# A recurrent attention block on one Trainium2 core: the order of gates and activations in its two halves

## The chip, the core and the metric

The kernel is one program on one core of a Trainium2 chip (trn2). The metric is the device time of one execution in microseconds (us), lower is better; the median of three executions before the change is 1480.96 us.

## The reference, cut to what matters

The whole program is a four-layer network on an input of 4 sequences of 256 tokens with 256 features. Each layer is a conditioning step, an attention block, another conditioning step and a feed-forward block. The change touches only the attention block of the second layer, which is a gated linear recurrence (RG-LRU) behind a causal convolution:

```python
def _rg_lru(x, wa, ba, wx, bx, lam):
    r = sigmoid(einsum('bld,ed->ble', x, wa) + ba)      # recurrence gate
    i = sigmoid(einsum('bld,ed->ble', x, wx) + bx)      # input gate
    log_a = -8.0 * r * softplus(lam)
    a = exp(log_a)
    mult = sqrt(maximum(1.0 - exp(2.0 * log_a), 0.0))
    b = mult * (i * x)
    # h[t] = a[t] * h[t-1] + b[t], along the sequence
# block: h = silu(x @ w1.T + b1); c = causal convolution of h with 4 taps, 320 -> 320 channels;
#        y = _rg_lru(c, ...) @ w2.T + b2;  x = x + y
```

The inner width is 320 channels. They are held as three channel groups of 128, 128 and 64 partitions.

## The kernel before, in words

The program is a chain of stages, one function per block of the network. Between two stages all engines meet. The stage of this case is `stage_l1_attn(l)` with l = 2; `stage_l1_ffn(3)` follows it. Each engine has its own instruction stream inside a stage, written out by hand; the streams meet only at semaphores, and every engine works strictly in the order written.

The 1024 tokens are two **halves** h = 0, 1 of 512 tokens (two sequences each), which fill one PSUM bank of 512 float32 columns. The unit of TensorE work is a `product`: one accumulation group into one bank, with one count of the semaphore `done` at its end. There are 28 of them, numbered by `group[0]`; product g uses bank g mod 8, so from g = 8 on it waits until ScalarE has evacuated product g - 8 (`evac` at least g - 7). In order:

- g 0 to 5: first projection w1, both halves, three channel groups each, 2 matmuls per product;
- g 6 to 11 (`G_CONV` = 6): the convolution, first half, then second half, 10 matmuls per product;
- g 12 to 23 (`G_GATE` = 12): the gates, per half and per channel group first the recurrence gate (`rec`), then the input gate (`inp`), 3 matmuls per product;
- g 24 to 27 (`G_OUT` = 24): the output w2, per half two blocks of 128 output features, 3 matmuls per product, behind `scan_ready`, which counts halves.

A float32 matmul of 512 columns stands in the trace as two instructions, so a convolution product is 20 of them, a gate or output product 6.

**ScalarE (ACT)** evacuates: Silu for w1 (L1122 to L1126), Identity into `conv` (L1135), Sigmoid into `rec` and `inp` (L1142). After all gates of both halves it computes, per half, three Exp into `mul` (L1149) and three Exp in place in `rec` (L1153), then for both halves three Sqrt each in `mul` (L1159). A change of function that needs another table puts an ACT_TABLE_LOAD in front.

**VectorE (DVE)** takes 1 minus (L1177) after the exponentials, then per half, behind `root_ready` and `ix_ready`, three products `mul` times `inp` (L1184) and six scans (L1189, the recurrence of 256 steps, one per channel group and sequence), and at the end four additions of output and bias to the residual `xT` (L1195).

**GpSimd (POOL)** multiplies gate and input, `inp` times `conv` (L1102), per half once all six gates of that half are evacuated.

Beside this the stage carries the work of the **next conditioning step**, 8 pieces of (128 features x 256 tokens). For each piece DVE computes `uk` and four scans (L151 to L158) and later a maximum, a reciprocal and a product (L192 to L198); ACT one Exp (`piece_act`, L169) behind DVE's `uk`; POOL two sums and a product (L175 to L180). DVE does them all (`block_dve`) before anything of the recurrence; ACT spreads its eight Exp over the six convolution evacuations. DVE's `uk` of piece i stands behind its `piece_finish` of piece i - 2, and two buffers take turns.

Of the kernel before, what the change touches and what calls it, by code (L numbers as in the profile page):

```python
# [14 lines left out]
P = 128  # L15
# [5 lines left out]
NP = CH * NB  # L21
# [18 lines left out]
ALU = mybir.AluOpType  # L40
ACT = mybir.ActivationFunctionType
# [49 lines left out]
def build_program(nc, io):  # L91
# [38 lines left out]
    dstep, astep, pstep = steps["dve"], steps["act"], steps["pool"]  # L130
# [6 lines left out]
    def vec(name, i=0):  # L137
        return vecs[:, ds(VEC[name][0] + i, 1)]
# [916 lines left out]
    def stage_l1_attn(l):  # L1055
        TP = T + 6
        RC = 3
        rows = (P, P, R1 - 2 * P)
        with ExitStack() as st:
            def sb(n, shape, dt=F32):  # L1060
# [13 lines left out]
            lam = sb("lam", [P, 6, RC])  # L1074
            ps = st.enter_context(nc.psum_tensor("R_ps", [P, 8, HALF], F32))
            names = ("ld_w1 ld_conv ld_gate ld_w2 zeroed done evac lam_ln "
                     "lam_ready a2_ready one_minus root_ready ix_ready scan_ready out_read").split()
            s = {n: sem("R_" + n) for n in names}
            block = st.enter_context(nc.Block())
            G_CONV, G_GATE, G_OUT = 6, 12, 24  # L1080
            h512 = lambda h: slice(h * HALF, (h + 1) * HALF)

            @block.sync
# [7 lines left out]
            @block.gpsimd  # L1091
            def _(pool):
                pool.memset(hid[:, :, :, :], 0.0)
                pstep.link(pool.memset(hid2[:, :, :], 0.0))
                pstep.link(pool.memset(conv[64:P, 2, :], 0.0))
                pool.memset(inp[64:P, 2, :], 0.0).then_inc(s["zeroed"], 1)
                block_pool(pool, l + 1)
                for h in range(2):
                    pool.wait_ge(s["evac"], G_GATE + 6 * (h + 1))
                    for f in range(RC):  # L1100
                        n = rows[f]
                        ins = pool.tensor_tensor(inp[0:n, f, h512(h)], inp[0:n, f, h512(h)], conv[0:n, f, h512(h)], ALU.mult)  # L1102
                        if f == RC - 2:
                            pstep.link(ins)
                    ins.then_inc(s["ix_ready"], 1)
                    pool.wait_ge(s["ix_ready"], h + 1)

            @block.scalar
            def _(act):
                condition_act(act, sig)  # L1110

                astep.link(act.activation(lam[:, 0, :], vecs[:, VEC["lam"][0]:VEC["lam"][0] + RC], ACT.Abs))
                astep.link(act.activation(lam[:, 1, :], lam[:, 0, :], ACT.Exp, scale=-1.0))
                act.activation(lam[:, 2, :], lam[:, 1, :], ACT.Ln, bias=1.0).then_inc(s["lam_ln"], 1)
                act.wait_ge(s["zeroed"], 1)
                pair = lambda x: x.rearrange("p (b t) -> p b t", b=2)
                for h in range(2):
# [11 lines left out]
                for h in range(2):  # L1129
                    for f in range(RC):  # L1130
                        g, n = G_CONV + 3 * h + f, rows[f]
                        for i in range(NP * (g - G_CONV) // 6, NP * (g - G_CONV + 1) // 6):
                            piece_act(act, l + 1, i, i % 2)
                        act.wait_ge(s["done"], g + 1)
                        act.activation(conv[0:n, f, h512(h)], ps[0:n, g % 8, :], ACT.Identity,  # L1135
                                       bias=vec("convb", f)[0:n, :]).then_inc(s["evac"], 1)
                for h in range(2):
                    for f in range(RC):
                        for j, (dst, b) in enumerate(((rec, "ba"), (inp, "bx"))):
                            g, n = G_GATE + 6 * h + 2 * f + j, rows[f]  # L1140
                            act.wait_ge(s["done"], g + 1)
                            act.activation(dst[0:n, f, h512(h)], ps[0:n, g % 8, :], ACT.Sigmoid,  # L1142
                                           bias=vec(b, f)[0:n, :]).then_inc(s["evac"], 1)
                act.wait_ge(s["lam_ready"], 1)
                act.wait_ge(s["evac"], G_OUT)
                for h in range(2):
                    for f in range(RC):
                        n = rows[f]
                        astep.mark(act.activation(mul[0:n, f, h512(h)], rec[0:n, f, h512(h)], ACT.Exp, scale=lam[0:n, 5, f:f + 1]))  # L1149
                    astep.wait()  # L1150
# [3 lines left out]
                    ins.then_inc(s["a2_ready"], 1)  # L1154
                for h in range(2):
                    act.wait_ge(s["one_minus"], h + 1)
                    for f in range(RC):
                        n = rows[f]
                        ins = act.activation(mul[0:n, f, h512(h)], mul[0:n, f, h512(h)], ACT.Sqrt, bias=1.0)  # L1159
                    ins.then_inc(s["root_ready"], 1)  # L1160
                next_sigmoid(act, l + 1)

            @block.vector
            def _(dve):
# [8 lines left out]
                for h in range(2):  # L1173
# [5 lines left out]
                for h in range(2):  # L1179
                    dve.wait_ge(s["root_ready"], h + 1)  # L1180
                    dve.wait_ge(s["ix_ready"], h + 1)
                    for f in range(RC):
                        n = rows[f]
                        dstep.link(dve.tensor_tensor(mul[0:n, f, h512(h)], mul[0:n, f, h512(h)], inp[0:n, f, h512(h)], ALU.mult))  # L1184
                    for f in range(RC):
                        n = rows[f]
                        for b in (2 * h, 2 * h + 1):
                            c = slice(b * T, (b + 1) * T)
                            ins = dve.tensor_tensor_scan(inp[0:n, f, c], rec[0:n, f, c], mul[0:n, f, c], 0.0, ALU.mult, ALU.add)  # L1189
                    ins.then_inc(s["scan_ready"], 1)  # L1190
# [8 lines left out]
            def _(pe):  # L1199
                group = [0]  # L1200

                def product(pairs, n):

                    g = group[0]
                    group[0] += 1
                    if g >= 8:
                        pe.wait_ge(s["evac"], g - 7)
                    for i, (w, x) in enumerate(pairs):
                        ins = pe.matmul(ps[0:n, g % 8, :], w, x, start=(i == 0), stop=(i == len(pairs) - 1))
                    ins.then_inc(s["done"], 1)  # L1210
# [14 lines left out]
                pe.wait_ge(s["ld_gate"], 16)  # L1225
                for h in range(2):
                    pe.wait_ge(s["evac"], G_CONV + 3 * (h + 1))
                    for f in range(RC):
                        c = slice(f * P, f * P + rows[f])
                        for j in range(2):  # L1230
                            product([(wgate[:, j, k, c], conv[:, k, h512(h)]) for k in range(RC)], rows[f])
                pe.wait_ge(s["ld_w2"], 16)
                for h in range(2):
                    pe.wait_ge(s["scan_ready"], h + 1)
                    for m in range(CH):
                        product([(w2[:, k, m * P:(m + 1) * P], inp[:, k, h512(h)]) for k in range(RC)], P)

    def stage_l1_ffn(l):  # L1240
# [879 lines left out]
```

## Time and profile before

| | |
|---|---|
| executions before | 1476.59, 1480.96, 1480.99 us; median 1480.96 |
| profiled execution, its own time | 1482.23 us |
| its span, first to last instruction | 1480.4 us |
| mean granted TensorE clock | 0.911 of 2.4 GHz |
| busy: PE, DVE, ACT, POOL | 79%, 66%, 40%, 39% of the span |
| the stage of this case | from 582.4 to 716.1 us of the span |

All times in views are microseconds from the start of the span. A view of windows gives busy time and instruction count of each engine in each stretch, and PEclk, the granted TensorE clock as a share of 2.4 GHz, where 0.50 is the lower of its two levels, 1.2 GHz. A timeline lists instructions in order of time with like neighbours merged: start, length, engine, line, operation, count, and in brackets how long the engine had been idle and who released it. A busy share over the whole span is a mean over stages with different limits.

### The profile page before, as it was taken

The page shows a single profiled execution, that of the slowest core. Times are in us where ns is not written, and L with a number is a line of the kernel's source. Part 1 is how long each engine was busy: PE and PEld are TensorE (multiplying, and loading weights), DVE is VectorE, ACT ScalarE, POOL GpSimd, SP SyncE. Part 2 cuts the span into 40 slices and gives each one's busy share as a digit, 9 for nine tenths or more (in the row PEclk, how much of TensorE's full clock was granted, in tenths as well). Part 3 has the DMA queues.
Part 4 walks back from the last instruction along what each step waited for, and adds up shares of the span by engine and source line. Part 5 has one row for each costly group of instructions (what it writes and reads, how often), then busy time and mean ns, then how long its engine had stood idle before and what let it go on. Part 6 is the DMA issues. An engine that isn't in the chain of part 4 may idle for free. (4 is left out here: it accounts for less than half of the span.)

```text
span 1480.4 us, 16753 instructions
## 1 busy us (share of the span) xinstructions
PE 1166.2 (79%) x5816; PEld 847.8 (57%) x5816; DVE 980.0 (66%) x1934; ACT 593.0 (40%) x1405; POOL 583.7 (39%) x462
## 2 busy tenths in 40 slices
PE   0177898989788887994779963999999966069997
PEld 0044555555557665431568853888888832047876
DVE  7757777877738987662513444888888858964345
ACT  2145556555635545225124522333333335123333
POOL 4346656565605651432051233444444411504520
PEclk9978999999979999997669995999999987569999
DMA  1121121021111102000423522110000000011101
GB/s 65 46 57 46 34 65 43 20 75 29 30 30 43 36 22 89 25 1 0 183 85 131 189 70 77 36 37 30 29 29 29 4 12 24 0 30 50 51 22 61
DMA packets 28979, 71.65 MB, mean 48 GB/s; under 512 B 4960, under 2 KB 14688, under 8 KB 26080
## 3 DMA queue, kind: packets, MB, share of 16 engines
q1 hardware_dynamic: 26320, 65.34, 14.4%
q0 software_dynamic: 1536, 4.20, 1.0%
q8 instruction: 47, 0.77, 0.2%
q10 hardware_dynamic: 1040, 1.05, 0.2%
q14 instruction: 36, 0.29, 0.1%
HBM read 55.89 MB, written 4.19 MB: 41 GB/s over the span
## 5 line engine op out<-in xcount | busy, mean ns | idle before, releaser
L175 POOL TENSOR_TENSOR sums<-scans 128x512 f32<-128x512 f32 x64 | 86.1, 1345 | 327.9 <-DVE scans L158 189.8
L504 ACT ACTIVATE probs<-ps_s,stats 128x256 f32<-128x256 f32 (+1 forms) x256 | 104.3, 419 | 102.2 <-DVE stats L571 102.1
L665 PE MATMUL ps_p<-xin,wkvq 128*128 128x512 f32 x148 | 75.9, 638 | 69.4 <-DMA wkvq<-w_l0a_dram 69.4
L450 POOL TENSOR_TENSOR probs<-probs,stats 128x512 f32<-128x512 f32 x64 | 67.5, 1055 | 127.8 <-DVE stats L577 127.8
L195 DVE RECIPROCAL sums<-sums 128x256 f32<-128x256 f32 x64 | 112.1, 1751 | 1.8
L571 DVE CUSTOM_DVE_ANT_0 ps_s<-ps_s,mask 128x256 f32<-128x256 f32 (+1 forms) x256 | 83.5, 387 | 23.9 <-PE ps_s L691 23.8
L180 POOL TENSOR_TENSOR sums<-sums,terms 128x512 f32<-128x512 f32 x64 | 86.7, 1355 | 4.4
L839 POOL TENSOR_TENSOR L3hid<-L3hid,L3sig 128x1024 f32<-128x1024 f32 x17 | 46.1, 2718 | 87.6 <-ACT L3sig L892 49.8
L665 PEld LDWEIGHTS ps_p<-xin,wkvq 128*128 128x128 f32 x148 | 26.9, 202 | 89.5 <-DMA wkvq<-w_l0a_dram 67.0
L1723 PE MATMUL K_ps_kvp<-K_wqkv_hi,K_xin_hi 128*128 128x256 f32 x256 | 75.1, 293 | 0.0
L1723 PE MATMUL K_ps_kvp<-K_wqkv_lo,K_xin_hi 128*128 128x256 f32 x256 | 72.5, 283 | 0.0
L1723 PE MATMUL K_ps_kvp<-K_wqkv_hi,K_xin_lo 128*128 128x256 f32 x256 | 72.4, 283 | 0.0
L1628 ACT ACTIVATE K_ks<-K_ps_kvp 128x256 f32<-128x256 f32 x64 | 24.7, 385 | 110.1 <-PE K_ps_kvp L1723 110.1
L701 PE MATMUL ps_t<-ident,probs 128*128 128x128 f32 x128 | 38.7, 302 | 37.0 <-ACT probT L511 23.0
L169 ACT ACTIVATE terms<-uk 128x256 f32<-128x256 f32 x64 | 26.5, 417 | 97.6 <-DVE uk L151 97.5
L691 PE MATMUL ps_s<-kr,qr 64*128 64x256 f32 (+1 forms) x512 | 61.5, 361 | 4.0 <-DVE qr L565 2.1
L717 PEld LDWEIGHTS ps_o<-probT,vtok 128*64 128x64 f32 x512 | 32.0, 140 | 49.5 <-issue 31.0
L1489 PE MATMUL E_ps<-E_dT,E_fc 128*128 128x256 f32 x256 | 59.1, 392 | 0.8 <-ACT E_dT L1344 0.8
L958 DVE TENSOR_TENSOR L3hid<-L3actg,L3ps_u 128x512 f32<-128x512 f32 x34 | 23.3, 687 | 54.4 <-ACT L3actg L886 54.4
L451 POOL TENSOR_TENSOR probs<-probs,stats 128x256 f32<-128x256 f32 x64 | 59.0, 923 | 0.0
L717 PE MATMUL ps_o<-probT,vtok 128*64 128x256 f32 (+1 forms) x512 | 57.6, 347 | 0.7 <-ACT oT L519 0.7
L691 PEld LDWEIGHTS ps_s<-kr,qr 64*128 64x128 f32 x512 | 45.9, 194 | 20.4 <-issue 10.9
(377 smaller groups left out, 3563.0 us busy)
## 6 DMA issues: line engine op xcount, KB each, us to landing
E_fc<-l_fc_dram SPq DMA_DIRECT2D x16, 1024.0 KB, 6.6
qswap<-qraw SPq DMA_DIRECT2D x64, 128.0 KB, 2.3
K_wqkv<-l_wqkv_dram SPq DMA_DIRECT2D x16, 384.0 KB, 3.3
L3wgu<-L_w_dram SPq DMA_DIRECT2D x17, 256.0 KB, 2.6
L0wgu<-L_w_dram SPq DMA_DIRECT2D x14, 256.0 KB, 2.6
wkvq<-w_l0a_dram SPq DMA_DIRECT2D x4, 768.0 KB, 4.5
L3wdn<-L_w_dram SPq DMA_DIRECT2D x17, 128.0 KB, 2.0
wo<-w_l0a_dram SPq DMA_DIRECT2D x4, 512.0 KB, 3.8
```

Source lines behind the costliest of these rows:

```text
L175: pstep.mark(pool.tensor_tensor(sums[:, k, :, :], scans[:, k, :, 0, :], scans[:, k, :, 1, :], ALU.add))
L180: pool.tensor_tensor(sums[:, k, :, :], sums[:, k, :, :], terms[:, k, :, :], ALU.add).then_inc(sums_ready, 1)
L195: dstep.mark(dve.reciprocal(den, den))
L450: pool.tensor_tensor(p1, p1, rs[:, 0:2].unsqueeze(2).to_broadcast([P, 2, T]), ALU.mult)
L451: pool.tensor_tensor(p0, p0, rs[:, 2:4].unsqueeze(2).to_broadcast([P, 2, P]), ALU.mult).then_inc(s["norm_done"], 1)
L504: ins = act.activation(dst[:, i % 2, :], src[:, i % 2, :], ACT.Exp, bias=stats[:, g % 4, 4 + i:5 + i], scale=-1.0, accum_out=stats[:, g % ...
L571: ins = dve.tensor_tensor_reduce(out=view, in0=view, in1=m, scale=-1.0, scalar=-NEG, op0=ALU.add, op1=ALU.min, accum_out=stats[:, g % 4, 4 ...
L665: ins = pe.matmul(ps[:, :], w[:, k, :], xin[:, k, h * HALF:(h + 1) * HALF], start=(k == 0), stop=(k == CH - 1))
L691: ins = pe.matmul(view[:, r, :], qr[h, (4 * c + m) % 2, b * T + tile * P:b * T + tile * P + P], kr[h, c % 2, b, 0:n], start=True, stop=True)
L717: ins = pe.matmul(o, vtok[:, c % 2, 2 * b + key, 64 * r:64 * r + 64], probT[:, g % 2, r, 0:256] if key == 0 else probT[:, g % 2, r, 256:38 ...
L1489: ins = pe.matmul(ps[:, h, i * CAP:(i + 1) * CAP], fc1[:, k, c, f:f + P], dT[:, c, ds(e * CAP, CAP)], start=(c == 0), stop=(c == CH - 1))
L1723: ins = pe.matmul(ps_kvp[:, h, a, :], x[:, k, t:t + P], w[:, j // 2, k, P:3 * P], start=(k + m == 0), stop=(k == CH - 1 and m == 2))
```

## The change

All of it lies in `stage_l1_attn`.

- TensorE: after the convolution of half 0 come the six gate products of half 0, then the convolution of half 1 and its gates. Within a half the three recurrence gates lead and the three input gates follow. `G_CONV` becomes (6, 15), `G_GATE` (9, 18). The first output product of each half waits for the scans channel group by channel group.
- ScalarE: the same order, with the exponentials of half 0 (`powers`) and its square roots (`roots`) placed among the evacuations of half 1's convolution. In half 1 the exponentials come after the recurrence gates and ahead of the input gates. The eight Exp of the conditioning pieces are spread from the start of the stage to the end of half 0's gates. Each square root counts for itself in `root_ready`.
- GpSimd: its multiplications go; VectorE does them (`inp` times `conv`), after 1 minus. VectorE handles half 0 wholly, then half 1; product and scans alternate per channel group, each group counting in `scan_ready`.

```diff
@@ GpSimd
                 block_pool(pool, l + 1)
-                for h in range(2):
-                    pool.wait_ge(s["evac"], G_GATE + 6 * (h + 1))
-                    for f in range(RC):
-                        n = rows[f]
-                        ins = pool.tensor_tensor(inp[0:n, f, h512(h)], inp[0:n, f, h512(h)], conv[0:n, f, h512(h)], ALU.mult)
...
@@ ScalarE
+                def gates(h, j):
+                    dst, b = ((rec, "ba"), (inp, "bx"))[j]
                     for f in range(RC):
+                        g, n = G_GATE[h] + RC * j + f, rows[f]
                         act.wait_ge(s["done"], g + 1)
+                        act.activation(dst[0:n, f, h512(h)], ps[0:n, g % 8, :], ACT.Sigmoid,
+                                       bias=vec(b, f)[0:n, :]).then_inc(s["evac"], 1)
+                def powers(h):
+                    act.wait_ge(s["lam_ready"], 1)
+                    act.wait_ge(s["evac"], G_GATE[h] + RC)
                     for f in range(RC):
                         n = rows[f]
+                        ins = act.activation(mul[0:n, f, h512(h)], rec[0:n, f, h512(h)], ACT.Exp, scale=lam[0:n, 5, f:f + 1])
+                    ins.then_inc(s["a2_ready"], 1)
+                    act.wait_ge(s["a2_ready"], h + 1)
                     for f in range(RC):
                         n = rows[f]
                         ins = act.activation(rec[0:n, f, h512(h)], rec[0:n, f, h512(h)], ACT.Exp, scale=lam[0:n, 4, f:f + 1])
+                    ins.then_inc(s["a_ready"], 1)
+                def roots(h):
                     act.wait_ge(s["one_minus"], h + 1)
                     for f in range(RC):
                         n = rows[f]
+                        act.activation(mul[0:n, f, h512(h)], mul[0:n, f, h512(h)], ACT.Sqrt, bias=1.0).then_inc(s["root_ready"], 1)
+                next_piece(0)
+                first(0)
+                next_piece(1)
+                first(1)
+                next_piece(2)
+                for f in range(RC):
+                    convolved(0, f)
+                    next_piece(3 + f)
+                gates(0, 0)
+                next_piece(6)
+                gates(0, 1)
+                next_piece(7)
+                powers(0)
+                convolved(1, 0)
+                convolved(1, 1)
+                roots(0)
+                convolved(1, 2)
+                gates(1, 0)
+                powers(1)
+                gates(1, 1)
+                roots(1)
                 next_sigmoid(act, l + 1)
@@ VectorE, for each half h, behind the 1 minus of that half
+                    dve.wait_ge(s["evac"], G_GATE[h] + 2 * RC)
                     for f in range(RC):
                         n = rows[f]
+                        ins = dve.tensor_tensor(inp[0:n, f, h512(h)], inp[0:n, f, h512(h)], conv[0:n, f, h512(h)], ALU.mult)
+                    dstep.link(ins)
+                    dve.wait_ge(s["a_ready"], h + 1)
                     for f in range(RC):
                         n = rows[f]
+                        dve.wait_ge(s["root_ready"], RC * h + f + 1)
+                        dstep.link(dve.tensor_tensor(mul[0:n, f, h512(h)], mul[0:n, f, h512(h)], inp[0:n, f, h512(h)], ALU.mult))
                         for b in (2 * h, 2 * h + 1):
                             c = slice(b * T, (b + 1) * T)
                             ins = dve.tensor_tensor_scan(inp[0:n, f, c], rec[0:n, f, c], mul[0:n, f, c], 0.0, ALU.mult, ALU.add)
+                        ins.then_inc(s["scan_ready"], 1)
@@ TensorE, for each half h, behind the convolution products of that half
+                    pe.wait_ge(s["evac"], G_CONV[h] + RC)
+                    for j in range(2):
+                        for f in range(RC):
+                            c = slice(f * P, f * P + rows[f])
                             product([(wgate[:, j, k, c], conv[:, k, h512(h)]) for k in range(RC)], rows[f])
                 pe.wait_ge(s["ld_w2"], 16)
                 for h in range(2):
                     for m in range(CH):
+                        if m == 0:
+                            pe.wait_ge(s["evac"], G_OUT + 2 * h + m - 7)
+                            for k in range(RC):
+                                pe.wait_ge(s["scan_ready"], RC * h + k + 1)
+                                ins = pe.matmul(ps[:, (G_OUT + 2 * h) % 8, :], w2[:, k, 0:P], inp[:, k, h512(h)],
+                                                start=(k == 0), stop=(k == RC - 1))
+                            ins.then_inc(s["done"], 1)
+                            group[0] += 1
+                        else:
+                            product([(w2[:, k, m * P:(m + 1) * P], inp[:, k, h512(h)]) for k in range(RC)], P)
```

## Rows read from the trace of the kernel before

**Rows 1.** Windows over the stage: length, busy us (instructions) of PE, PEld, DVE, ACT, POOL, PEclk, DMA
```profile
598.80:650.90 52.10, 52.10 (x122) 20.15 (x120) 42.50 (x51) 8.63 (x16) 28.13 (x24) 1.00 0.00 1
650.90:682.60 31.70, 31.61 (x73) 12.04 (x72) 2.47 (x3) 9.56 (x14) 4.37 (x4) 1.00 0.00 1
682.60:701.20 18.60, 0.00 (x0) 0.01 (x1) 7.92 (x16) 15.59 (x23) 3.75 (x3) 0.61 0.00 0
701.20:715.70 14.50, 13.57 (x24) 5.56 (x24) 8.42 (x13) 0.00 (x0) 0.00 (x0) 0.79 0.00 0
```
**Rows 2.** Waits in the stage: us in total, times, longest one
```profile
DVE R_mul L1177 <- ACT R_rec L1153: 37.2, 2, 34.5
```
**Rows 3.** Timeline from the last gate to the next stage
```profile
682.55 0.68 ACT L1142 ACTIVATE R_inp<-R_ps,vecs 64x512 f32<-64x512 f32 x1 [1.89 <-PE R_ps L1209]
683.31 1.28 ACT L1149 ACT_TABLE_LOAD   x1
683.38 3.83 POOL L1102 TENSOR_TENSOR R_inp<-R_inp,R_conv 128x512 f32<-128x512 f32 x3 [12.03 <-ACT R_inp L1142]
684.61 1.95 ACT L1149 ACTIVATE R_mul<-R_rec,R_lam 128x512 f32<-128x512 f32 x3
686.59 1.95 ACT L1153 ACTIVATE R_rec<-R_rec,R_lam 128x512 f32<-128x512 f32 x3
...
690.40 1.94 ACT L1153 ACTIVATE R_rec<-R_rec,R_lam 128x512 f32<-128x512 f32 x3
692.36 1.28 ACT L1159 ACT_TABLE_LOAD   x1
692.38 1.09 DVE L1177 TENSOR_SCALAR R_mul<-R_mul 128x512 f32<-128x512 f32 x3 [2.73 <-ACT R_rec L1153]
693.66 3.23 ACT L1159 ACTIVATE R_mul<-R_mul 128x512 f32<-128x512 f32 x6
695.36 2.13 DVE L1184 TENSOR_TENSOR R_mul<-R_mul,R_inp 128x512 f32<-128x512 f32 x3 [1.89 <-ACT R_mul L1159]
...
697.53 3.59 DVE L1189 TENSOR_TENSOR_SCAN R_inp<-R_rec,R_mul 128x256 f32<-128x256 f32 x6
...
701.22 13.57 PE L1209 MATMUL R_ps<-R_inp,R_w 128*128 128x512 f32 x24 [18.71 <-issue]
...
714.90 0.75 DVE L1195 SCALAR_TENSOR_TENSOR xT<-R_ps,vecs,xT 128x512 f32<-128x512 f32 x1 [1.82 <-PE R_ps L1209]
716.13 0.33 SPq L1282 DMA_DIRECT2D E_wgate<-l_wg_dram  x1
```
**Rows 4.** Timeline of ACT and PE: where products of convolution and gates are evacuated
```profile
624.88 0.68 ACT L1135 ACTIVATE R_conv<-R_ps,vecs 64x512 f32<-64x512 f32 x1 [7.43 <-PE R_ps L1209]
...
642.24 0.69 ACT L1135 ACTIVATE R_conv<-R_ps,vecs 128x512 f32<-128x512 f32 x1 [7.59 <-PE R_ps L1209]
...
650.86 31.65 PE L1209 MATMUL R_ps<-R_conv,R_wgate 128*128 128x512 f32 x72
...
650.97 0.68 ACT L1135 ACTIVATE R_conv<-R_ps,vecs 64x512 f32<-64x512 f32 x1 [7.43 <-PE R_ps L1209]
653.74 0.69 ACT L1142 ACTIVATE R_rec<-R_ps,vecs 128x512 f32<-128x512 f32 x1 [0.79 <-PE R_ps L1209]
...
669.53 0.69 ACT L1142 ACTIVATE R_rec<-R_ps,vecs 128x512 f32<-128x512 f32 x1 [2.09 <-PE R_ps L1209]
```
**Rows 5.** Timeline of DVE: the last instruction of the conditioning pieces
```profile
653.66 0.42 DVE L198 TENSOR_TENSOR mod<-sums 128x256 f32<-128x256 f32 x1
```
**Rows 6.** Pauses of PE in other stages: one matmul behind a pause; windows as in rows 1
```profile
515.04 0.47 PE L1010 MATMUL L0ps_g<-L0xin_hi,L0wgu_hi 128*128 128x512 f32 x1 [1.72 <-DVE L0hid L958]
...
510.00:520.00 10.00, 8.28 (x37) 6.59 (x36) 9.70 (x13) 5.30 (x7) 5.77 (x4) 1.00 0.08 26
1192.00:1198.00 6.00, 3.10 (x19) 2.36 (x18) 5.29 (x12) 0.00 (x0) 1.68 (x2) 1.00 0.00 0
1199.00:1200.00 1.00, 0.00 (x0) 0.00 (x0) 1.00 (x3) 1.00 (x1) 0.00 (x0) 0.50 0.00 0
```

More of the change, by code:

```diff
@@ L1076, in stage_l1_attn @@
             names = ("ld_w1 ld_conv ld_gate ld_w2 zeroed done evac lam_ln "
-                     "lam_ready a2_ready one_minus root_ready ix_ready scan_ready out_read").split()
+                     "lam_ready a2_ready a_ready one_minus root_ready scan_ready").split()
             s = {n: sem("R_" + n) for n in names}
             block = st.enter_context(nc.Block())
-            G_CONV, G_GATE, G_OUT = 6, 12, 24
+            G_CONV, G_GATE, G_OUT = (6, 15), (9, 18), 24
             h512 = lambda h: slice(h * HALF, (h + 1) * HALF)
@@ L1116, in _, with first @@
                 pair = lambda x: x.rearrange("p (b t) -> p b t", b=2)
-                for h in range(2):
+                def first(h):
                     for f in range(RC):
@@ L1128, in _, with convolved @@
                         ins.then_inc(s["evac"], 1)
-                for h in range(2):
+                def convolved(h, f):
+                    g, n = G_CONV[h] + f, rows[f]
+                    act.wait_ge(s["done"], g + 1)
+                    act.activation(conv[0:n, f, h512(h)], ps[0:n, g % 8, :], ACT.Identity,
+                                   bias=vec("convb", f)[0:n, :]).then_inc(s["evac"], 1)
+                def gates(h, j):
+                    dst, b = ((rec, "ba"), (inp, "bx"))[j]
@@ L1130, in _ @@
                     for f in range(RC):
-                        g, n = G_CONV + 3 * h + f, rows[f]
-                        for i in range(NP * (g - G_CONV) // 6, NP * (g - G_CONV + 1) // 6):
-                            piece_act(act, l + 1, i, i % 2)
+                        g, n = G_GATE[h] + RC * j + f, rows[f]
                         act.wait_ge(s["done"], g + 1)
-                        act.activation(conv[0:n, f, h512(h)], ps[0:n, g % 8, :], ACT.Identity,
-                                       bias=vec("convb", f)[0:n, :]).then_inc(s["evac"], 1)
@@ L1137, in _ @@
[L1137 to L1144, printed above, removed]
@@ L1145, in _ @@
-                act.wait_ge(s["evac"], G_OUT)
-                for h in range(2):
+                        act.activation(dst[0:n, f, h512(h)], ps[0:n, g % 8, :], ACT.Sigmoid,
[3 more added lines that the diff above has]
+                    act.wait_ge(s["evac"], G_GATE[h] + RC)
                     for f in range(RC):
                         n = rows[f]
-                        astep.mark(act.activation(mul[0:n, f, h512(h)], rec[0:n, f, h512(h)], ACT.Exp, scale=lam[0:n, 5, f:f + 1]))
-                    astep.wait()
+                        ins = act.activation(mul[0:n, f, h512(h)], rec[0:n, f, h512(h)], ACT.Exp, scale=lam[0:n, 5, f:f + 1])
+                    ins.then_inc(s["a2_ready"], 1)
+                    act.wait_ge(s["a2_ready"], h + 1)
@@ L1153, in _ @@
                         ins = act.activation(rec[0:n, f, h512(h)], rec[0:n, f, h512(h)], ACT.Exp, scale=lam[0:n, 4, f:f + 1])
-                    ins.then_inc(s["a2_ready"], 1)
-                for h in range(2):
+                    ins.then_inc(s["a_ready"], 1)
+                def roots(h):
                     act.wait_ge(s["one_minus"], h + 1)
@@ L1158, in _, with next_piece @@
                         n = rows[f]
-                        ins = act.activation(mul[0:n, f, h512(h)], mul[0:n, f, h512(h)], ACT.Sqrt, bias=1.0)
-                    ins.then_inc(s["root_ready"], 1)
+                        act.activation(mul[0:n, f, h512(h)], mul[0:n, f, h512(h)], ACT.Sqrt, bias=1.0).then_inc(s["root_ready"], 1)
+                def next_piece(i):
+                    piece_act(act, l + 1, i, i % 2)
+                next_piece(0)
[19 more added lines that the diff above has]
+                roots(1)
                 next_sigmoid(act, l + 1)
@@ L1178, in _ @@
                     ins.then_inc(s["one_minus"], 1)
-                for h in range(2):
-                    dve.wait_ge(s["root_ready"], h + 1)
-                    dve.wait_ge(s["ix_ready"], h + 1)
+                    dve.wait_ge(s["evac"], G_GATE[h] + 2 * RC)
                     for f in range(RC):
                         n = rows[f]
-                        dstep.link(dve.tensor_tensor(mul[0:n, f, h512(h)], mul[0:n, f, h512(h)], inp[0:n, f, h512(h)], ALU.mult))
+                        ins = dve.tensor_tensor(inp[0:n, f, h512(h)], inp[0:n, f, h512(h)], conv[0:n, f, h512(h)], ALU.mult)
+                    dstep.link(ins)
+                    dve.wait_ge(s["a_ready"], h + 1)
                     for f in range(RC):
                         n = rows[f]
+                        dve.wait_ge(s["root_ready"], RC * h + f + 1)
+                        dstep.link(dve.tensor_tensor(mul[0:n, f, h512(h)], mul[0:n, f, h512(h)], inp[0:n, f, h512(h)], ALU.mult))
                         for b in (2 * h, 2 * h + 1):
@@ L1189, in _ @@
                             ins = dve.tensor_tensor_scan(inp[0:n, f, c], rec[0:n, f, c], mul[0:n, f, c], 0.0, ALU.mult, ALU.add)
-                    ins.then_inc(s["scan_ready"], 1)
+                        ins.then_inc(s["scan_ready"], 1)
                 for h in range(2):
@@ L1224, in _ @@
                                 + [(wconv[:, 8 + q, c], hid2[:, b, 4 * q:4 * q + T]) for q in range(2)], rows[f])
[L1225 to L1230, printed above, removed]
+                    if h == 0:
+                        pe.wait_ge(s["ld_gate"], 16)
+                    pe.wait_ge(s["evac"], G_CONV[h] + RC)
+                    for j in range(2):
+                        for f in range(RC):
+                            c = slice(f * P, f * P + rows[f])
                             product([(wgate[:, j, k, c], conv[:, k, h512(h)]) for k in range(RC)], rows[f])
@@ L1233, in _ @@
                 for h in range(2):
-                    pe.wait_ge(s["scan_ready"], h + 1)
                     for m in range(CH):
-                        product([(w2[:, k, m * P:(m + 1) * P], inp[:, k, h512(h)]) for k in range(RC)], P)
+                        if m == 0:
[8 more added lines that the diff above has]
+                            product([(w2[:, k, m * P:(m + 1) * P], inp[:, k, h512(h)]) for k in range(RC)], P)
     def stage_l1_ffn(l):
```

4 lines of the change are left out of this document (removed).

## The prediction, made before the changed kernel was run

> **What bounds the kernel now.** A mean over the span (TensorE 79% busy) says nothing about one stage, so I cut the stage into windows first [rows 1]. TensorE is full through the convolution (52.10 of 52.10 us) and the gates (31.61 of 31.70 us) at the full clock; then it does nothing for 18.60 us, and works 13.57 us on the output. So the stage is TensorE work with one hole, and the last 33 us are what can be won. The view of waits says what the other engines do meanwhile: VectorE waits 34.5 us for the first exponentials of the recurrence [rows 2], although half 0's gates were evacuated long before. The timeline gives the chain in the hole [rows 3]: last Sigmoid at 682.55, table load, four groups of three Exp, table load, square roots, three VectorE products, six scans, TensorE from 701.22, last addition 714.90 to 715.65, next stage's first issue 716.13. ACT is busy 15.59 of the 18.60 us [rows 1]. TensorE's 24 output instructions begin at the lower clock (PEclk 0.79 over that window).
>
> **The change, part by part.** I follow one chain: TensorE up to the last gate, then ACT, VectorE, TensorE, VectorE. Everything is counted in the profiled execution's own clock.
>
> *Moved products: two new stalls.* Before, the next product starts 0.11 us ahead of ACT's evacuation of the one before it (650.86 against 650.97 [rows 4]). After, half h's first gate product waits for the evacuation of that half's last convolution product: 0.68 us [rows 4] and a handoff, 0.10 us as between the scans' end 701.12 and TensorE at 701.22 [rows 3]. So 0.11 + 0.68 + 0.10 = 0.89 us, twice: 1.78 us. Bounds: 0.7 (no handoff) to 1.5 us each. The first stall is at 624.88, the second near 667.7. The last gate product is thus evacuable at 682.55 + 1.78 = 684.33.
>
> *Recurrence gates lead.* Six gate products take 669.53 - 653.74 = 15.79 us [rows 4], three take 7.90. The third recurrence gate of half 1 is evacuated from 684.33 - 7.90 = 676.43 to 677.11.
>
> *Exponentials under the input gates.* A change of table took 683.23 to 684.61, 1.38 us; the other (692.34 to 693.66) 1.32; two groups of three Exp start 1.98 apart and the last takes 1.95 [rows 3]. So Exp runs from 678.49, second group 680.47 to 682.42. The change adds a third switch on the way, back to Sigmoid: 683.74. The first two input gates are ready by then; three Sigmoid at the 0.62 us spacing of the Exp end at 684.98 + 0.68 = 685.66. VectorE's 1 minus (1.09 us) starts at 680.47 and is hidden beneath this.
>
> *Roots and input products side by side.* The roots start 1.32 later, 686.98, the first is done at 687.59. GpSimd's 3.83 us for three `inp` times `conv` [rows 3] go; before they lay beside Exp and cost nothing. On VectorE I price them by the nearest row, L1184, 2.13 us for three of the same shape [rows 3]: 685.68 to 687.81. Bounds: 1.8 us (no pause between them) to 3.83 (no faster than GpSimd). Before they were free, now they are on the path.
>
> *Products and scans per group.* Three products and six scans took 695.36 to 701.12, 5.76 us, 1.92 per channel group [rows 3]; order within does not alter the sum. From 687.85: 689.77, 691.69, 693.61. The later roots, 0.52 us apart, are ahead.
>
> *Output.* TensorE does half 0's two output products, 12 instructions of 0.44 us (31.65 us for 72 [rows 4]), straight after the gates, by about 689.5, and four of half 1's first product as their groups arrive. After 693.71 eight instructions are left. At the full clock VectorE's last addition starts about 8 x 0.44 + 0.22 = 3.74 us later, 697.45, and ends at 698.20.
>
> *Half 0* lies under half 1's convolution and gates, which is the cover for six Exp, three roots, input products, products and scans; without it they would cost a second such tail. Its 1 minus comes after VectorE's conditioning pieces, done at 654.08 [rows 5], so by 655.2. ACT reaches `roots(0)` after evacuating the second product of half 1's convolution, 642.24 + 0.89 + 15.79 + 0.69 = 659.61 [rows 4]. They end about 662.6. The third is due at 650.97 + 0.89 + 15.79 = 667.65, so nothing is late.
>
> *ACT's pieces.* They start earlier and bring nine more table loads in all, 17 for 8, nearly all in ACT's idle time between products (7.43 us before L1135 [rows 4]). Beside TensorE's 52.10 us of convolution ACT is busy 8.63 [rows 1]. The two pieces among the first evacuations delay them by up to some 3 us, but the convolution of half 0 needs only the first three, which the first piece hardly moves. Cost 0, at most 1 us. No DMA is added or moved.
>
> **Sum.** End of the stage 715.65 becomes 698.20: 17.4 us less. The profiled execution's own time is 1482.23 (span 1480.4 and 1.8 around it), so 1464.8; against the median of 1480.96, 1463.6. The later stages shift whole.
>
> **A rule that speaks against it.** In the rows the ACTIVATE starts 0.02 us behind its table load, and the load 0.02 to 0.08 us behind the ACTIVATE before it [rows 3]. The Trainium skill (ScalarE: Activation LUTs, What ACT_TABLE_LOAD costs) puts a switch at about 2.66 us, load and drain together, and (Rules for kernel authors) says to do all of one set before switching. With 2.66 in place of 1.38 and 1.32 the tail would be some 3.7 us longer. The rows show only half that price, so the rule on order stands, but at 1.3 us per switch, of which only one more is on the path.
>
> **The rivals.**
>
> *A. The clock falls in the tail.* While TensorE waits for half 1's scans it works about 1.8 us in the 4.2 between 689.5 and 693.7. For: in another stage 3.10 us of work in 6.00 ended with the clock at 0.50 one microsecond later [rows 6]. Against: a single pause of 1.72 us left it at 1.00 over the window of 10 us around it [rows 6]; the two new stalls of 0.9 us are less still. If it falls the last eight instructions take up to twice as long, 3.5 us: 1467.1.
>
> *B. Switches back and forth cost more than those seen.* The trace has no Sigmoid right behind Exp in this chain; if each of the three costs another load's 1.28 us [rows 3], the roots come 2 x 1.28 later, the first root another 1.28, of which 0.2 is hidden: 3.6 us later, 1467.2. The skill's drain (same section) would be this mechanism. The two switches in the rows speak against it.
>
> *C. No change.* That needs 13 us of the 17.4 back. The change would have to fail at its purpose: half 0's recurrence not done by 684, so that its scans join the tail with 5.76 us, its roots and input products with some 6, and a clock already low, with 2 to 3 more. It takes `one_minus` of half 0 about 20 us late. 1476 to 1481.
>
> *D. Slower: VectorE late for `one_minus(0)`.* The new wait stands in ACT ahead of the last convolution evacuation, behind which all gates of half 1, and TensorE with them, are queued. The pieces' last products are VectorE's entry to it. They may be late by 667.65 - 3.0 - 655.2 = 9.5 us at no cost, beyond it one for one; from 9.5 + 17.4 = 26.9 us late the change loses. At 40 us late: 1494. Against: before, ACT releases the last two pieces after the evacuation of 642.24 [rows 4]; after, the seventh about 634 and the eighth behind half 0's input gates, about 642.2. VectorE is busy 42.50 of 52.10 us in that window [rows 1], not much denser after.
>
> **How the numbers follow.** A measurement of this kernel can tell about 0.3%, 4.4 us, from no change. Chances: the forecast 0.60, with half a microsecond either way in its terms; A 0.26; B 0.04; some unlisted loss that leaves 5 to 13 us, 0.04; C 0.03; D 0.03. Faster 0.94, same 0.03, slower 0.03. Range: the low end takes free stalls (1.8), cheap input products (0.3) and part of the spread of the three runs (1476.59 is 4.4 under the median), 1458; the high end takes A or B with input products at GpSimd's price (1.7), 1470.
>
> **What would show it.** Per step in the profile after: TensorE idle about 0.9 us before the first gates of each half; no idle of over 2 us between the last gate and the stage's end; three pauses near 0.8, 1.0, 1.0 us before half 1's scans; third recurrence gate to first Exp 1.4 us; ACT_TABLE_LOAD x17 in the stage; VectorE's L1184 of half 0 before 665; four additions with the last about 14 us behind the last gate's evacuation; next stage's first issue near 698.7. PEclk of 0.50 in the last 4 us says A. A gap between ACTIVATE and load says B. `roots(0)` waiting for VectorE past 665 says D. The prediction is wrong if the next stage starts later than 705 or an equal time is lost elsewhere.

## The result and the profile after

| | before | after |
|---|---|---|
| median of four executions each, us | 1478.78 (1475.97 to 1480.99) | 1460.76 (1458.43 to 1463.96) |
| ratio, 95% interval | | 0.9869 [0.9849, 0.9889] |
| profiled execution: own time, span, clock | 1482.23, 1480.4, 0.911 | 1458.67, 1456.6, 0.922 |
| first convolution matmul to next stage's first activation | 598.78 to 716.23 = 117.45 | 593.78 to 694.02 = 100.24 |

The change is faster by 18.0 us between the medians; 17.4 were forecast, the time as 1463.6 in 1458 to 1470. The median itself is 2.8 us below the forecast, and 2.2 of these come from the kernel before, whose median went from 1480.96 to 1478.78 with a fourth execution. The spans of the two profiled executions differ by 23.8 us, and the last line of the table says how much of that is the change: 17.21 us. The other 6.6 lie outside the rewritten order. The stage's first matmul came 3.6 us earlier on its span's clock (581.95 against 585.55), the first projection took 11.83 us instead of 13.23 (its granted clock was 0.88 instead of 0.78), and the stages behind took 762.6 instead of 764.2. A second profiled execution of the changed kernel (`d1_changed_again` below) shows that most of this does not belong to the change: the stretch was 100.23 again, but the stage's first matmul came at 584.03, the projection took 13.46 us and the stages behind 763.9. So the readings below are taken from this stretch.

The windows of the kernel after, columns as in [rows 1]: the first runs from the convolution to the last gate, the second to the end of the stage's work.

```profile
593.80:679.80 86.00, 84.41 (x193) 31.86 (x191) 50.79 (x71) 36.16 (x51) 22.79 (x20) 1.00 0.00 1
679.80:693.90 14.10, 11.34 (x25) 4.23 (x24) 10.45 (x16) 5.63 (x9) 0.00 (x0) 1.00 0.00 0
```

The first window is 2.2 us longer than its two counterparts before (52.10 + 31.70) and no longer full (TensorE is busy 84.41 of 86.00 us); ACT works 36.16 us in it instead of 18.2. The second replaces 33.1 us [rows 1, 3]. TensorE's clock stays up in it.

The timeline of the kernel after, from the last but three evacuations of half 1 on, answers to [rows 3]:

```profile
671.87 0.68 ACT L1133 ACTIVATE R_rec<-R_ps,vecs 64x512 f32<-64x512 f32 x1 [2.03 <-PE R_ps L1229]
672.63 1.28 ACT L1141 ACT_TABLE_LOAD   x1
673.93 1.95 ACT L1141 ACTIVATE R_mul<-R_rec,R_lam 128x512 f32<-128x512 f32 x3
675.90 1.95 ACT L1146 ACTIVATE R_rec<-R_rec,R_lam 128x512 f32<-128x512 f32 x3
677.87 1.28 ACT L1133 ACT_TABLE_LOAD   x1
679.16 1.83 ACT L1133 ACTIVATE R_inp<-R_ps,vecs 128x512 f32<-128x512 f32 x3
681.01 1.28 ACT L1153 ACT_TABLE_LOAD   x1
682.30 1.67 ACT L1153 ACTIVATE R_mul<-R_mul 128x512 f32<-128x512 f32 x3
...
679.83 2.84 PE L1259 MATMUL R_ps<-R_inp,R_w 128*128 128x512 f32 x6
682.51 2.74 PE L1229 MATMUL R_ps<-R_inp,R_w 128*128 128x512 f32 x6
685.21 1.10 PE L1259 MATMUL R_ps<-R_inp,R_w 128*128 128x512 f32 x2
687.01 1.13 PE L1259 MATMUL R_ps<-R_inp,R_w 128*128 128x512 f32 x2 [0.70 <-DVE R_inp L1209]
688.88 1.13 PE L1259 MATMUL R_ps<-R_inp,R_w 128*128 128x512 f32 x2 [0.75 <-DVE R_inp L1209]
...
681.02 1.89 DVE L1200 TENSOR_TENSOR R_inp<-R_inp,R_conv 128x512 f32<-128x512 f32 x3 [4.03 <-ACT R_inp L1133]
683.07 0.69 DVE L1206 TENSOR_TENSOR R_mul<-R_mul,R_inp 128x512 f32<-128x512 f32 x1 [0.15 <-ACT R_mul L1153]
692.69 0.75 DVE L1215 SCALAR_TENSOR_TENSOR xT<-R_ps,vecs,xT 128x512 f32<-128x512 f32 x1 [1.65 <-PE R_ps L1229]
```

Read it as one chain: recurrence gate, Exp, Sigmoid, Sqrt on ACT without a gap of over 0.1 us; VectorE takes over at 681.02 and 683.07; TensorE starts half 1's first channel group without a pause and waits 0.70 us for the second and 0.75 for the third. The last gate product ends at 679.8, and from there it is 14.2 us to the next stage's activation. But the chain leaves TensorE earlier, at the third recurrence gate: from its evacuation at 671.87 on ACT is never idle for over 0.1 us, and the last gate product has ended before the third of ACT's three Sigmoids, which start 0.6 us apart from 679.16, needs it.

The timeline of TensorE after shows the price, to be read beside [rows 4]: two pauses, and gates that take 16.1 us for six products. ACT's timeline shows how a further table load can cost nothing: the load at 663.66 is done while ACT would have to wait for TensorE anyway.

```profile
620.66 16.17 PE L1229 MATMUL R_ps<-R_conv,R_wgate 128*128 128x512 f32 x36 [0.82 <-issue]
636.76 26.16 PE L1229 MATMUL R_ps<-R_hid,R_wconv 128*128 128x512 f32 x60
663.70 16.20 PE L1229 MATMUL R_ps<-R_conv,R_wgate 128*128 128x512 f32 x36 [0.77 <-ACT R_conv L1125]
...
663.66 1.28 ACT L1133 ACT_TABLE_LOAD   x1
666.58 0.69 ACT L1133 ACTIVATE R_rec<-R_ps,vecs 128x512 f32<-128x512 f32 x1 [1.63 <-PE R_ps L1229]
```

### The profile page after: what moved, and what is told of

It is laid out like the page before. It is cut to its first block and busy times, and to the rows that moved or that the text cites. A ratio compares the mean times of both kernels' runs of the same rounds, so it can differ in the third digit from the quotient of the medians.

```text
span 1456.6 us, 16761 instructions
## 1 busy us (share of the span) xinstructions
PE 1157.8 (79%) x5816; PEld 842.7 (58%) x5816; DVE 981.5 (67%) x1940; ACT 604.5 (42%) x1414; POOL 576.3 (40%) x456
```

## The experiments

In all of them M is the stretch from the first convolution matmul to the first activation of the next stage: 117.45 us before, 100.24 after. Each was profiled once, and most have a single device time. Such a time does not rank kernels this close: the mirrored gates below have an M 0.35 us below the changed kernel's, yet their one execution took 1465.0 us, longer than any of the changed kernel's nine (1458.43 to 1464.65).

### One part undone at a time

**Both convolutions first.**

```diff
-            G_CONV, G_GATE, G_OUT = (6, 15), (9, 18), 24
+            G_CONV, G_GATE, G_OUT = (6, 9), (12, 18), 24
@@ TensorE, the gate loop, now behind both convolutions
-                    if h == 0:
-                        pe.wait_ge(s["ld_gate"], 16)
+                pe.wait_ge(s["ld_gate"], 16)
+                for h in range(2):
@@ ScalarE, the new order, behind the evacuations of both convolutions with pieces 3 to 7 between them (the lines that go are left out)
                 gates(0, 0)
+                powers(0)
                 gates(0, 1)
                 roots(0)
                 gates(1, 0)
                 powers(1)
                 gates(1, 1)
                 roots(1)
```

> The changed kernel, but TensorE does both convolutions before the gates, as before the change; ScalarE follows, with the half-0 recurrence placed under half 0's input gates and half 1's gates. Everything else of the change stays. Measured is the stretch from the first convolution matmul to the first activation of the next stage: 117.45 us before, 100.24 after. Theory (the gain is the shorter chain behind the last gate, wherever half 0 is hidden; the new order only costs two stalls of 0.84 us): 98.6, since both stalls go and half 0's recurrence still fits under half 1's gates. Rival (the gain comes from half 0's gates following their convolution on TensorE): ScalarE has too little room under the gates, the tail grows, 104 or more.

M = 98.54. So the place of half 0's gates on TensorE is not what wins: with both convolutions first again (within a half the recurrence gates still lead), the new order of ACT and VectorE wins 1.7 us more, the price of the two stalls. The timeline of ACT in this kernel shows half 0's exponentials and roots fitting between the evacuations of its own gates and of half 1's, without an idle gap:

```profile
662.04 1.95 ACT L1146 ACTIVATE R_rec<-R_rec,R_lam 128x512 f32<-128x512 f32 x3
664.00 1.28 ACT L1133 ACT_TABLE_LOAD   x1
665.30 1.83 ACT L1133 ACTIVATE R_inp<-R_ps,vecs 128x512 f32<-128x512 f32 x3
667.15 1.28 ACT L1153 ACT_TABLE_LOAD   x1
668.44 1.67 ACT L1153 ACTIVATE R_mul<-R_mul 128x512 f32<-128x512 f32 x3
670.13 1.28 ACT L1133 ACT_TABLE_LOAD   x1
671.43 1.27 ACT L1133 ACTIVATE R_rec<-R_ps,vecs 128x512 f32<-128x512 f32 x2
```

**Gates in pairs.**

```diff
@@ TensorE and ScalarE: the gate loops
-                    for j in range(2):
-                        for f in range(RC):
+                    for f in range(RC):
+                        for j in range(2):
@@ ScalarE, half 1
-                gates(1, 0)
+                gates(1)
                 powers(1)
-                gates(1, 1)
```

> The changed kernel, but recurrence and input gate of each channel group follow each other as before, so that all exponentials of a half come after all its gates. Theory: no third table switch, but two groups of three Exp lie bare in the tail while the input products are hidden; last gate evacuated about 680.0 on the changed kernel's clock, Exp to 685.3, square roots from 686.6, scans end at 693.0 where they ended at 688.8: stretch 104.4 us. It also has two changes of width of a gate product fewer per half, 0.3 us each half, which is in that number. Rival (the third switch costs as much as leading with the recurrence gates wins): 100 to 101.

M = 105.66, 1.3 us over the expectation. The chain is as worked out: last gate product's end to scans' end is 13.9 us (683.4 to 697.3) instead of 9.0, and the gates end 0.68 us earlier. The rest is TensorE's clock: from the scans' end to the last addition's end it is 5.78 us instead of 4.61. TensorE's timeline has a pause of 4.89 us, and behind it twelve instructions that begin slowly:

```profile
693.71 5.75 PE L1257 MATMUL R_ps<-R_inp,R_w 128*128 128x512 f32 x6 [4.89 <-DVE R_inp L1207]
699.25 3.01 PE L1227 MATMUL R_ps<-R_inp,R_w 128*128 128x512 f32 x6
```

**Input products on GpSimd.** GpSimd's loop of the old kernel is put back with its semaphore, and VectorE waits for that:

```diff
-                    dve.wait_ge(s["evac"], G_GATE[h] + 2 * RC)
...
+                    dve.wait_ge(s["ix_ready"], h + 1)
```

> The changed kernel, but GpSimd multiplies input gate and convolution as before. Theory: in half 1 it starts 0.15 us behind the last Sigmoid and takes 3.83 us, to about 685.0, where VectorE was done at 682.9 and the first root at 682.9: 1.9 us later, stretch 102.1. Rival (hidden beneath the square roots, as before the change): 100.2.

M = 102.81. The products are bare here: GpSimd starts at 686.27 and ends at 690.10, and VectorE starts its first product 0.04 us later. That makes 1.9 us of the 2.6; the other 0.7 is the clock again, which fell behind a pause of 1.90 us, 1.1 us of work and a pause of 0.70 us. Timeline of this kernel:

```profile
686.27 3.83 POOL L1102 TENSOR_TENSOR R_inp<-R_inp,R_conv 128x512 f32<-128x512 f32 x3 [34.63 <-ACT R_inp L1142]
690.14 0.69 DVE L1211 TENSOR_TENSOR R_mul<-R_mul,R_inp 128x512 f32<-128x512 f32 x1 [8.01 <-POOL R_inp L1102]
692.28 1.10 PE L1264 MATMUL R_ps<-R_inp,R_w 128*128 128x512 f32 x2 [1.90 <-DVE R_inp L1214]
694.08 3.64 PE L1264 MATMUL R_ps<-R_inp,R_w 128*128 128x512 f32 x4 [0.70 <-DVE R_inp L1214]
```

**Scans and output by half.**

```diff
@@ VectorE: three products, then six scans; TensorE: one wait per half
+                    for f in range(RC):
                         for b in (2 * h, 2 * h + 1):
...
-                                pe.wait_ge(s["scan_ready"], RC * h + k + 1)
+                    pe.wait_ge(s["scan_ready"], h + 1)
```

> The changed kernel, but VectorE does three products and then six scans, and TensorE's output waits for a whole half. Theory: product and scan time is the same in sum, and after the last scan TensorE has 12 instructions instead of 8, 1.7 us: stretch 102.0 with TensorE's clock at 2.4 GHz. Now TensorE does nothing for 3.7 us ahead of them. Rival (the waits per group also keep the clock up): the clock falls in that pause and the 12 instructions take up to twice as long, stretch 102.5 to 107.

M = 103.63, 3.39 more: 1.74 for the four further instructions behind the last scan (4 x 0.434), which leaves 1.65 for the clock. It went down just as TensorE came back and stayed down for some 3.4 us, and half the speed over that time costs about as much. The windows of this kernel:

```profile
688.00:690.00 2.00, 0.00 (x0) 0.00 (x0) 2.00 (x4) 0.00 (x0) 0.00 (x0) 1.00 0.00 0
690.00:691.00 1.00, 0.19 (x1) 0.19 (x2) 1.00 (x3) 0.00 (x0) 0.00 (x0) 0.90 0.00 0
691.00:694.00 3.00, 3.00 (x4) 1.32 (x5) 1.15 (x2) 0.00 (x0) 0.00 (x0) 0.50 0.00 0
694.00:697.00 3.00, 3.00 (x8) 1.26 (x7) 0.75 (x1) 0.00 (x0) 0.00 (x0) 0.96 0.00 0
```

### The order by itself, and one switch more

**Order alone**: the edits of the last three experiments (pairs, GpSimd, by half) together.

> Of the change only the order is left: half 0's gates behind its convolution and half 0's recurrence beneath half 1. The gates go in pairs, GpSimd multiplies the inputs, and scans and output wait for a half. Theory: TensorE ends the gates 85.4 us after the first convolution matmul, scans end 13.9 us later, twelve output instructions begin at the lower clock after 8 us of pause: stretch 109.0 us, so the order alone is worth some 8.4 of the 17.2 us and the other parts, which shorten the tail of half 1, the rest. Rival (the parts add up as they were priced singly, 5.4 + 2.6 + 3.4 us, on top of 100.24): 111.6.

M = 109.14. So of 17.2 us the order takes 8.3 and the other parts 8.9 together. Undone singly they cost 5.4 + 2.6 + 3.4 = 11.4: not a sum. The larger part of the difference of 2.5 us, 1.9 us, is that GpSimd's products are hidden again once the exponentials lie bare (they end at 687.7, VectorE's first product waits for the roots until 691.05). The rest is the clock, which is lost once, but for longer: behind the pause of 8.56 us it costs 2.9 us here, 3.5 in the three single runs together. So 2.9 of the 8.9 us are TensorE's clock. From the timeline of this kernel:

```profile
696.87 8.37 PE L1234 MATMUL R_ps<-R_inp,R_w 128*128 128x512 f32 x12 [8.56 <-DVE R_inp L1214]
```

**One switch more.**

```diff
                 powers(1)
+                act.activation(unread[:, 0:1], ident[:, 0:1], ACT.Sqrt)
                 gates(1, 1)
```

> The changed kernel with one idle activation more on ScalarE, a square root of one column, between half 1's exponentials and its input gates, so that one table switch more lies on the chain of the tail. Theory (a switch costs its load and 0.02 us): 1.30 for the load and about 0.2 for the activation, stretch 101.7 to 101.8 us, if TensorE's clock stays up; the pause ahead of half 1's output grows by 1.5 us, to about 2.3, and with it up to 3.5 us more if the clock falls, which PEclk shows. Rival (a switch costs about twice its load): 103.1 or more with the clock up, and a gap between the activations and the loads.

M = 102.55. From the timeline of this kernel the two loads are 1.51 us apart, the activation 0.20 of it, with gaps of 0.02 or less:

```profile
681.01 1.28 ACT L1177 ACT_TABLE_LOAD   x1
682.31 0.20 ACT L1177 ACTIVATE unread<-ident 128x1 f32<-128x1 f32 x1
682.52 1.28 ACT L1133 ACT_TABLE_LOAD   x1
683.81 1.83 ACT L1133 ACTIVATE R_inp<-R_ps,vecs 128x512 f32<-128x512 f32 x3
...
689.86 1.10 PE L1260 MATMUL R_ps<-R_inp,R_w 128*128 128x512 f32 x2 [1.46 <-DVE R_inp L1210]
691.66 3.81 PE L1260 MATMUL R_ps<-R_inp,R_w 128*128 128x512 f32 x4 [0.70 <-DVE R_inp L1210]
```

The 0.8 us beyond 1.5 is the clock: four instructions take 3.81 us in the last row, where at the full clock two take 1.13, and PEclk is 0.50 from 692 to 695. The pause of 1.46 us stands ahead of the first channel group, where the changed kernel has none; there the clock stayed.

### What the change left behind

**Gate waits per group.** The first gate product of each half waits inside its loop, and the loop over the gates leaves it out:

```diff
-                    pe.wait_ge(s["evac"], G_CONV[h] + RC)
+                    for k in range(RC):
+                        pe.wait_ge(s["evac"], G_CONV[h] + k + 1)
+                        ins = pe.matmul(ps[:, g % 8, :], wgate[:, 0, k, 0:P], conv[:, k, h512(h)],
+                                        start=(k == 0), stop=(k == RC - 1))
```

> The changed kernel, but the first gate product of each half waits for the evacuated convolution channel group by channel group, so that its first two matmuls (1.7 us) cover the evacuation of the third group. Theory: both stalls of 0.84 us vanish, stretch 98.5 to 98.6. Rival (the stall only moves behind the second matmul): 99.5 or more.

M = 98.53. Both stalls are gone.

**Output products per group.** In half 1 the loop over the channel groups k is outside, over the output blocks m inside; half 0 waits for its three groups at once.

```diff
+                for k in range(RC):
+                    pe.wait_ge(s["scan_ready"], RC + k + 1)
+                    for m in range(CH):
+                        ins = pe.matmul(ps[:, (G_OUT + 2 + m) % 8, :], w2[:, k, m * P:(m + 1) * P], inp[:, k, h512(1)],
+                                        start=(k == 0), stop=(k == RC - 1))
...
```

> The changed kernel, but in half 1 both output products take each channel group as its scans come, so that 4 instructions instead of 8 are left after the last scan. Theory: 4 x 0.434 = 1.74 us less, stretch 98.5; the pauses of TensorE shrink to 0.1 us each. Rival (VectorE's additions, now closer together behind the scans, take it back): 99.2 to 100.

M = 98.62: 1.62 of the 1.74. VectorE's four additions now run without a pause.

**Mirrored gates.** TensorE's loop; ScalarE evacuates in the same order.

```diff
-                        for f in range(RC):
+                        for f in (range(RC) if j == 0 else range(RC - 1, -1, -1)):
```

> The changed kernel, but the three input gates of each half run from the third channel group to the first, so that the two gate products of 64 output rows stand next to each other, as they did before the change. Theory: in the traces a product behind one of another width is ready 0.14 us later than usual (128 to 64 rows) and 0.19 us (64 to 128); the change has one such pair more per half, so six gate products take 15.8 us again instead of 16.1, and the stretch is 99.6 us. Rival (the 0.3 us belongs to the restart behind the stall): 100.2 and 16.1 us as in the changed kernel.

M = 99.89; the six gate products of half 1 take 15.90 us (668.02 to 683.92), those of half 0 15.86 (625.33 to 641.19). So 0.24 of the 0.34 us per half goes. The other 0.1 is seen one step on: half 1's convolution, from its start to its first gate product, takes 26.83 us here, behind a gate of 128 rows, and 26.94 in the changed kernel and in the pairs, behind one of 64. Half 0's gates and that convolution together take 42.69 us here, 42.70 in the pairs and 43.04 in the changed kernel, so all of half 0's 0.35 us goes with the order of widths.

That is also all that M gains. Half 1's own 0.23 us lies among its input gates, behind the third recurrence gate, where ACT and no longer TensorE carries the chain: from the start of the convolution to VectorE's 1 minus of half 1 it is 81.78 us here and 82.12 in the changed kernel, and the tail behind it is as long in both. So the expectation priced 0.3 us too much.

**Joined**, and the changed kernel beside them on the same chip.

> Both convolutions ahead of the gates, mirrored gates, and output products per channel group, in one kernel. Theory: 100.24 less 1.70, 0.66 and 1.62 us, stretch 96.3, and 4 us under the changed kernel in device time. Rival (with 15.8 us for six gates ScalarE, which needs four table switches in them, becomes the chain): 97 or more.

> The changed kernel's order with gate waits per channel group, mirrored gates, and output products per channel group. Theory: 100.24 less 1.71, 0.66 and 1.62 us, stretch 96.3. Rival (the parts hide each other): 97 or more.

> The changed kernel itself beside the others, on the same chip. Theory: stretch 100.2 again, and 17 to 18 us under the kernel before; outside the stretch the executions differ by up to 5 us with the moments at which TensorE's clock changes, in both kernels alike.

| | M | device time, median (range), executions | to before, 95% interval |
|---|---|---|---|
| before, same chip | not profiled | 1480.64 (1475.21 to 1483.32), 9 | |
| changed kernel | 100.23 | 1463.33 (1459.64 to 1464.65), 5 | 0.9883 [0.9860, 0.9906] |
| joined, convolutions first | 96.58 | 1460.74 (1459.68 to 1461.57), 4 | 0.9872 [0.9848, 0.9895] |
| joined, waits per group | 96.58 | 1460.63 (1458.74 to 1461.27), 4 | 0.9870 [0.9847, 0.9894] |

In the stretch the joined kernels beat the changed one by 3.65 us. That is 0.3 less than expected, by the mirrored gates' over-priced 0.66, and just what the parts gave singly (1.70 + 0.35 + 1.62 = 3.67). In device time the medians say 2.6 and 2.7 where 4 was expected, with ranges that overlap, so a gain of the whole program over the changed kernel is not shown. Timeline of the second at its end; the pauses of TensorE are down to 0.3 us and less:

```profile
682.75 5.31 PE L1230 MATMUL R_ps<-R_inp,R_w 128*128 128x512 f32 x12
688.37 5.66 PE L1269 MATMUL R_ps<-R_inp,R_w 128*128 128x512 f32 x12 [0.30 <-DVE R_inp L1210]
...
691.91 3.08 DVE L1216 SCALAR_TENSOR_TENSOR xT<-R_ps,vecs,xT 128x512 f32<-128x512 f32 x4
```

## Why the prediction was right, and where its terms were off

- **Sum.** Forecast for this stretch 17.4 us, measured 17.21. The forecast took the profiled execution's gain over to the median, which moved by 18.0; the difference lies within the spread of executions. The mechanism is the forecast one step by step, but that the sum comes within 0.24 us is in part luck. On the clock of the kernel before (the stretch starts 5.00 us earlier after), the third recurrence gate of half 1 was evacuated at 677.55 where 677.11 was forecast, 0.44 us late; the input products gave 0.24 back.
- **Stalls.** 0.89 us each forecast, 0.84 measured (26.88 us from convolution to gates for 26.04). But TensorE's part, to the last gate product's end, grew by 2.4 us (83.73 to 86.12), not 1.78: the gate products of a half take 16.10 us instead of 15.8. That the recurrence gates' lead also alternates widths was not priced: pairs in place of it end the gates 0.68 us earlier.
- **Input products.** 2.13 us forecast, 1.89 measured, as 0.63 each when none waits for the one before. Their start waited for the last Sigmoid, as forecast, and the first square root and their end (682.91) fall together.
- **Third switch.** 1.32 forecast, 1.29 to 1.30 measured. Rival B is refuted, by the gaps in the changed kernel and by the added switch. In the tail's rows after, no load stands more than 0.08 us behind its ACTIVATE. So the 2.66 us per switch of the Trainium skill (ScalarE: Activation LUTs, What ACT_TABLE_LOAD costs) is not what these traces show; one more switch on the chain cost its load, 1.28 us, and the activation. The stage has 17 loads, as counted.
- **Products, scans, output.** 5.76 us forecast for scans and products, 683.07 to 688.83 measured, 5.76. From there to the last addition's end 4.59 forecast (693.61 to 698.20), 4.61 measured.
- **Pauses.** Three were named, near 0.8, 1.0 and 1.0 us, though the forecast's own times (689.5 and 689.77) leave about 0.4 for the first. There are two, 0.70 and 0.75 us, and none ahead of the first group: half 0's output products run until 685.2, and that group's scans end at 685.06.
- **Rival A**, the clock, did not come true in either profiled execution of the changed kernel, but its mechanism is real and near. Four experiments put a single pause of 1.46, 1.90, 3.64 or 4.89 us ahead of half 1's output, where the changed kernel has none before the first group; each lost 0.7 to 1.65 us to the clock on top, and the order alone, with 8.56 us, lost 2.9. Of the profit of the waits per group and of VectorE's input products a part is that they keep the pauses short.
- **Rival D** was far: VectorE's 1 minus for half 0 ended at 646.2, ACT's square roots started at 656.2.
- **The reading of the change** was too kind in one point: the prediction put half 0 under half 1's convolution and took that cover for necessary. The first experiment shows that half 0's input gates and half 1's gates are cover enough without the convolution, and that this costs no stall.

## What to carry to other kernels

When an engine is idle at the end of a stage, ask which of its own results the chain behind it needs first, and let it make these first: the order of consumers on ScalarE and VectorE won here; half 0's gates ahead of half 1's convolution on TensorE did not. A group-wide wait in front of an accumulating product can be split by its reduction steps; the first steps then cover the evacuation of the last. In a tail with pauses, a microsecond or two added to a pause can cost another 0.7 to 1.65 us by the clock, as here, so price both. And a gain on TensorE counts only as far as TensorE carries the chain: behind the third recurrence gate it was worth nothing here.

## What the runs showed of the hardware that was not expected

- Clock: TensorE's pauses of 0.70 and 0.75 us between the channel groups of half 1's output, with 1.1 us of work between them, left PEclk at 1.00 in both executions. In one execution each, a first pause of 1.46 (one switch more) or 1.90 us (GpSimd), 1.1 us of work and a pause of 0.70 us were followed by PEclk 0.50 for some 3.4 us.
- Widths: a gate product behind one of another number of output rows is ready some 0.1 to 0.2 us later (2.72 and 2.77 us for 2.58 between evacuations); in the mirrored order 0.35 us came back, all of it in half 0's gates and the convolution behind them.
- A table load is hidden wholly where ACT would wait anyway (663.66 above, with 1.63 us of waiting left behind it): in the changed kernel the stage has 17 loads for 8, and on the chain only one more is seen.
